# Causal attention of a twelve-layer decoder: row sums from a widened value tile, and a new quotient

## The reference, cut to what matters

```python
q = (x @ Wq_w.T + Wq_b).reshape(b, t, h, s).transpose(0, 2, 1, 3)   # kk, v alike; h = 16, s = 16
dot = jnp.einsum('bhqd,bhkd->bhqk', q, kk)
dot = jnp.where(causal, dot, -jnp.inf) / jnp.sqrt(256.0)
attn = jax.nn.softmax(dot, axis=-1)
out = jnp.einsum('bhqk,bhkd->bhqd', attn, v).transpose(0, 2, 1, 3).reshape(b, t, k)
return out @ Wo_w.T + Wo_b            # then x = layernorm(x + that)
```

## Time and profile before

| what | us |
|---|---|
| median of 3 runs | 3064.9 |
| the profiled execution | 3043.24 |
| its span | 3041.4 |
| TensorE busy in the span | 2806.5 (92%) |
| VectorE busy in the span | 1905.0 (63%) |
| ScalarE busy in the span | 1218.6 (40%) |
| TensorE records of L769, 512, mean 345 ns | 28.9 after overlap |
| TensorE records of L773, 512, mean 338 ns | 28.1 after overlap |
| VectorE reciprocal L960, 8, mean 3350 ns | 26.8 |

### The profile page before, as it was taken

One profiled execution on the slowest core, in us unless ns is written; L12 is line 12 of the kernel. 1 busy time (PEld: TensorE's weight loads), 2 busy tenths in 40 slices (PEclk: granted clock), 3 DMA queues, 4 the chain that ended last, 5 costly groups with the idle time before them and its releaser, 6 DMA issues. The chain is left out here.

```text
span 3041.4 us, 52348 instructions
## 1 busy us (share of the span) xinstructions
PE 2806.5 (92%) x20888; PEld 1815.5 (60%) x20888; DVE 1905.0 (63%) x3430; ACT 1218.6 (40%) x2591; POOL 324.8 (11%) x459
## 2 busy tenths in 40 slices
PE   6999899999998979899999989899898899989898
PEld 3565456666666858566666667656565333346576
DVE  4675367777764347477777753345557999966522
ACT  1333254445542335355544431133242866633111
POOL 1111100000002700000000000000111000001232
PEclk9999999999999979899999999999999999999899
DMA  3001000000012331100000000100000000000241
GB/s 117 20 14 69 23 33 5 5 5 5 5 67 78 92 127 37 42 5 5 8 6 5 36 18 1 33 17 21 19 21 32 18 1 1 1 18 18 101 168 66
DMA packets 43246, 103.58 MB, mean 34 GB/s; under 512 B 4929, under 2 KB 32687, under 8 KB 39425
## 3 DMA queue, kind: packets, MB, share of 16 engines
q1 hardware_dynamic: 37217, 86.66, 8.1%
q0 software_dynamic: 5792, 13.59, 1.5%
HBM read 66.74 MB, written 19.07 MB: 28 GB/s over the span
## 5 line engine op out<-in xcount | busy, mean ns | idle before, releaser
L2350 ACT ACTIVATE prob<-R,neg_max 128x333 f32<-128x333 f32 x512 | 268.7, 538 | 184.0 <-DVE neg_max L2417 183.8
L3898 DVE TENSOR_TENSOR_SCAN arena<-arena,u 128x512 f32<-128x512 f32 x256 | 289.5, 1200 | 0.3 <-issue 0.2
L2238 PEld LDWEIGHTS T<-const,prob 128*128 128x128 f32 (+1 forms) x1536 | 183.6, 143 | 82.4 <-DVE prob L2430 37.0
L2430 DVE TENSOR_TENSOR prob<-prob,rec 128x666 f32<-128x666 f32 x256 | 218.4, 853 | 19.8 <-issue 0.9
L2417 DVE TENSOR_REDUCE neg_max<-R 128x2 f32<-128x666 f32 x256 | 205.8, 845 | 34.9 <-PE R L2227 34.8
L2238 PE MATMUL T<-const,prob 128*128 128x128 f32 (+1 forms) x1536 | 211.0, 274 | 13.0 <-DVE prob L2430 10.7
L2357 ACT ACTIVATE prob_t<-T 128x384 f32<-128x384 f32 x256 | 125.8, 491 | 228.4 <-PE T L2238 222.3
L3829 ACT ACTIVATE arena<-delta,neg_a 128x510 f32<-128x510 f32 x256 | 174.5, 714 | 40.2 <-DVE arena L3898 39.1
L2423 DVE COPY prob_t<-T 128x384 f32<-128x384 f32 x256 | 142.3, 556 | 39.5 <-PE T L2238 13.0
L2157 PE MATMUL O<-keys_in,arena 128*128 128x333 f32 x512 | 164.8, 444 | 0.0
L3732 PE MATMUL R<-arena,diag 64*64 64x512 f32 x1024 | 136.0, 620 | 27.4 <-DVE arena L3898 27.3
(11 more groups left out here) (590 smaller groups left out, 5341.6 us busy)
## 6 DMA issues: line engine op xcount, KB each, us to landing
w<-w_dram SPq DMA_DIRECT2D x16, 1024.0 KB, 6.9
arena<-pack_dram SPq DMA_DIRECT2D x2, 4100.0 KB, 14.6
q_pad<-q_pad SPq DMA_DIRECT2D x24, 224.0 KB, 2.7
arena<-pack_dram SPq DMA_DIRECT2D x4, 1284.0 KB, 6.6
arena<-pack_dram SPq DMA_DIRECT2D x1, 4896.0 KB, 15.3
slots_in<-x_nat SPq DMA_DIRECT2D x2, 2048.0 KB, 8.7
arena<-planes SPq DMA_DIRECT2D x8, 512.0 KB, 8.5
arena<-k_nat SPq DMA_DIRECT2D x16, 224.0 KB, 2.7
```

The source lines that it names most:

```text
L2238: last = nc.tensor.transpose(S.T[0:n, i, kc * P:(kc + 1) * P], prob[:, g % 2, i, first:first + n], S.ident)
L2350: last = nc.scalar.activation(prob[:, g % 2, i, :], S.R[:, g % 2, i * BANK:i * BANK + XK], ACT.Exp, bias=neg_max[:, g % 2, i:i + 1], accum ...
L2430: nc.vector.tensor_tensor(prob[:, g % 2, :, :], prob[:, g % 2, :, :], rec[:, g % 2, :].unsqueeze(2).to_broadcast([P, 2, XK]), ALU.mult)\
L3898: nc.vector.tensor_tensor_scan(state[:, q % HELD, :], decay[:, q % DEEP, :], u[:, i % 2, :], 0.0, ALU.mult, ALU.add)\
```

## The change

The value tile is set to 1.0 instead of 0.0 once, so that the 16 unused columns of each head's 32 are ones. The product of a head with its tile then gives its 16 features and, in the other 16 partitions, its row sum. Even heads go to one bank (`S_one`), odd heads to the other (`S_two`), since they can no longer add up in one. The eight matmuls with `ones2` per call go, and `ones2` with its three memsets. ScalarE gets a new step `halves(b)`, between `keys(i+1)` and exponentials 0: it copies `S_one` times the mask `even` to `own`. VectorE's `quotient` becomes: transpose `S_two` in blocks of 32 x 32 to `turned`; after `halves_sb`, transpose `S_one`; `S_two * odd + own` to `attn_t`, which frees both banks (`sums_read`); reciprocal of the 32 sums of each token; a transpose of them, repeated 16 times, to `rec`; multiply. The next batch's product waits for `sums_read` in place of `attn_ready`.

```diff
@@ product @@
                     if t == 0:
                         pe.wait_ge(M.v_sb, b + 1)
                         if b >= 1:
-                            pe.wait_ge(M.attn_ready, b)
+                            pe.wait_ge(M.sums_read, b)
...
-                for s in range(2):
+                for s, sums in enumerate((S_one, S_two)):
                     for j in range(4):
-                        nc.tensor.matmul(S_num[32 * j:32 * j + 32, at], v2[:, b % 2, kt, 8 * t + 2 * j + s, :], exps_of(kt, t, j, s),
-                                         start=(t == 0 and kt == 0 and s == 0), stop=(kt == 1 and s == 1), skip_group_check=True)
-                for s in range(2):
-                    for j in range(4):
-                        last = nc.tensor.matmul(S_den[32 * j:32 * j + 32, at], ones2[:, s, :], exps_of(kt, t, j, s),
-                                                start=(t == 0 and kt == 0 and s == 0), stop=(kt == 1 and s == 1), skip_group_check=True)
+                        last = nc.tensor.matmul(sums[32 * j:32 * j + 32, at], v2[:, b % 2, kt, 8 * t + 2 * j + s, :], exps_of(kt, t, j, s),
+                                                start=(t == 0 and kt == 0), stop=(kt == 1), skip_group_check=True)
@@ scalar @@
+            def halves(b):
+                act.wait_ge(M.pv_full, b + 1)
+                if b >= 1:
+                    act.wait_ge(M.sums_read, b)
+                nc.scalar.activation(own[:], S_one, ACT.Copy, scale=even).then_inc(M.halves_sb, 1)
...
                     keys(i + 1)
+                if 0 <= i - 2 < B:
+                    halves(i - 2)
                 if 0 <= i - 1 < B:
                     exps(i - 1, 0)
@@ vector @@
             def quotient(b):
                 dve.wait_ge(M.pv_full, b + 1)
-                nc.vector.reciprocal(rec[:], S_den)
-                dve.drain()
-                nc.vector.tensor_tensor(attn_t[:, b % 2, :, :].rearrange("p c t -> p (c t)"), S_num, rec[:], ALU.mult)\
-                    .then_inc(M.attn_ready, 1)
+                nc.vector.transpose(turned[:, 1, :], S_two)
+                dve.wait_ge(M.halves_sb, b + 1)
+                nc.vector.transpose(turned[:, 0, :], S_one)
+                shares = attn_t[:, b % 2, :, :].rearrange("p c t -> p (c t)")
+                nc.vector.scalar_tensor_tensor(shares, S_two, odd, own[:], ALU.mult, ALU.add).then_inc(M.sums_read, 1)
+                sums = turned[:].rearrange("p s n -> p (s n)")[:, 16:2 * BANK - 16].rearrange("p (s n) -> p s n", s=2)[:, :, 0:BANK - 31:32]
+                dve.drain()
+                nc.vector.reciprocal(inverse[:].rearrange("p n s -> p s n"), sums)
+                dve.drain()
+                nc.vector.transpose(rec[:].rearrange("p (n s m) -> p n s m", s=2, m=16), inverse[:].unsqueeze(3).to_broadcast([P, 16, 2, 16]))
+                dve.drain()
+                nc.vector.tensor_tensor(shares, shares, rec[:], ALU.mult).then_inc(M.attn_ready, 1)
...
-            nc.vector.memset(ones2[:], 0.0)
-            nc.vector.memset(v2[:], 0.0)
-            dve.drain()
-            for s in range(2):
-                nc.vector.memset(ones2[:, s, 16 * s:16 * s + 16], 1.0)
+            nc.vector.memset(v2[:], 1.0)
+            dve.drain()
```

More of the change, by code:

```diff
@@ L630, in causal16 @@
         rstd = sb("rstd_own", [P, 2, TT])
-        ones2 = sb("ones2", [P, 2, 32])
+        own = sb("own", [P, BANK])
+        turned = sb("turned", [P, 2, BANK])
+        inverse = sb("inverse", [P, 16, 2])
         bq_s = sb("bq_s", [P, C])
-        S_q, S_y, S_num, S_den = S.T[:, 0, :], S.T[:, 1, :], S.O[:, 0, :], S.O[:, 1, :]
+        S_q, S_y, S_one, S_two = S.T[:, 0, :], S.T[:, 1, :], S.O[:, 0, :], S.O[:, 1, :]
         def bank(j):
@@ L809, in _ @@
                 if i < 2:
-                    keep_warm(nc, S, S_num, 1 + i)
+                    keep_warm(nc, S, S_one, 1 + i)
                 if now:
@@ L824, in _ @@
                     if i < 2:
-                        keep_warm(nc, S, S_num, 1)
+                        keep_warm(nc, S, S_one, 1)
                     scores(i, 1)
@@ L868, in _ @@
             settle(pe, M.attn_ready, B)
+            settle(pe, M.sums_read, B)
             settle(pe, M.y_read, B)
@@ L938, in _ @@
             bv = part(W, TB, "bv").rearrange("p (g m) -> p g m", m=32)
+            odd = part(S.const, CONST, "odd")
             def maxima(b, f):
@@ L1010, in _ @@
             settle(dve, M.pv_full, B)
+            settle(dve, M.halves_sb, B)
             settle(dve, M.y_full, B)
```

## The result

The changed kernel takes 3053.9 us (median of 15 runs, 3042.3 to 3067.7) against 3066.3 for the kernel before (15 runs, 3056.6 to 3083.6). The ratio is 0.9964, 95% interval 0.9948 to 0.998: between 6 and 16 us less, 11 in the middle. Times in us compare only within one measurement: beside e1 to e4 the kernel before took 3047.2, beside e5 to e8 3069.2, beside e9 to e12 3048.3.

A forecast was written before the change was run, and what follows sets the result against it. TensorE's own work, ending last in gaps 1 and 5, was taken as the bound. Loop 6.1 plus drain 3.1 made 9.2 us, less 2.2 for the clock: 7.0 off 3064.9, forecast 3057.9, range 3053 to 3067.

The forecast's parts named there:

- the drain: End of the causal block: earlier product start and fewer ones matmuls save 3.1 us, range 2.3 to 3.1.
- rival 1: Whole kernel: the clock holds, so the full 9.2 us is gained, giving 3055.7; chance 0.22.
- its larger loop term: Gap 5 of iterations 1 and 2: upper bound, two times 0.9 us more gained, giving 3053.9.
- iterations 1 and 2, gaps 1 and 5: Early loop: 0.49 us gained in gap 1 of iteration 2, 0.9 in gap 5 of each iteration.
- Gaps 1, 3 and 5: Between the loop's score groups: 0.87, 0.86 and 0.86 us of TensorE work go; 0.49, nothing and 0.47 are gained.
- The hand-over after gap 1: From the end of the maxima to the next score group: at least 0.05 us, as in gap 3.
- Rival 2: Loop: something other than TensorE holds the next group back; only the drain gains, 3.1 us, 3061.8; chance 0.14.
- rival 3: Loop, such as gap 3: the clock falls often, 2.67 us per slow stretch; with five, 3069.9; chance 0.14.
- Gap 5 at half clock: Iterations 1 and 2: 0.9 us gained in each, 1.8 together, from bounds of 0.47 and 1.79 each.
- Quotient, copy, queues: VectorE's new quotient, ScalarE's 0.69 us copy and moved queues cost 0; the quotient has 0.55 us of cover.
- The clock: Slow stretches take back 2.2 us: 0.8 in the drain, 1.35 in the loop in iteration 3 or 7.
- the price 0 of gap 3: Gap 3 of the loop: 0.86 us of TensorE work becomes a wait for the maxima, gaining nothing.

The follow-up runs named there:

- e1: Changed kernel with every product matmul issued twice: 3040.6 us against 3047.2 for the kernel before, ratio 0.9988.
- e4: Changed kernel with eight pairs of idle matmuls where TensorE waits longest in the causal block: ratio to the kernel before 0.9945.
- e5: Kernel before, unchanged, timed against itself: ratio 0.9992.
- e8: Changed kernel with the transpose of the first bank made three times, a quotient 1.6 us longer: one execution, 3075.6 us.
- e9: Kernel of e4 with more idle matmuls ahead of the second and third batch's scores in the next block: 3031.8 us against 3048.3 before, ratio 0.9946.
- e12: Changed kernel, unchanged, run again for a fourth profile; no total time or ratio of its own is given.
- e2: Kernel before with the ones matmuls issued for batch 0 alone: 3041.1 us against 3047.2 before, ratio 0.998.
- e7: The kernel of e4 measured again: ratio to the kernel before 0.9969.
- e10: Kernel before with the idle matmuls of e4 in the same places: 3044.3 us against 3048.3 before, ratio 0.998.

## Why the prediction was right

The direction and the mechanism of the gaps and of the drain were right, and the time lies in the range, 0.9 above its lower end: 3053.9 for a forecast of 3057.9 and a range of 3053 to 3067. That it lies inside is in part luck. The gain by the ratio is 11 us, not 7.0, and about 3 of it belong to no term of the sum. The time is also what rival 1 gives with its larger loop term, 3053.9, although its condition, that the clock holds, was not met: here the number alone would have named the wrong case. And absolute times move more between measurements than the 0.2% that the chances took: the kernel before had medians from 3047.2 to 3069.2. By terms, means of three profiles before and four after:

```
step                                 forecast   measured
start of block and iteration 0          0        -1.6
iterations 1 and 2, gaps 1 and 5       -2.3      -2.3
iterations 1 and 2, elsewhere           0        +1.7
iterations 3 to 5                      -2.9      -2.7
iteration 6                            -1.0      -0.3
maxima 0 of batch 7 to exponentials 0   0        +0.6
last exponentials 0 to last quotient   -3.1      -3.1
clock, unplaced                        +2.2      (in the rows above)
block                                  -7.0      -7.8
```

- **Gaps 1, 3 and 5.** Right: 0.87 and 0.86 of TensorE's time go, 0.40 and 0.47 are gained, nothing in gap 3. The hand-over after gap 1 was taken from gap 3 as 0.05 and is 0.15, hence 0.87 a full iteration and not 0.96. Rival 2 falls with this: after both gaps the bracket names the maxima. Of rival 3, falls in iterations 3 to 6, one came, in iteration 6.
- **Gap 5 at half clock.** Right in size: 1.8 forecast for iterations 1 and 2, 1.12 + 0.82 = 1.9 measured from maxima 2 to the next maxima 0. (The middle of the lower half of its bounds is 0.8, not the 0.9 taken; it doesn't matter.)
- **The drain** is right to 0.01 (14.84 measured, 17.93 - 3.08 = 14.85 worked out). The first block's 15.63, taken as the bound, held a fall of the clock: the same stretch of that block takes 14.77 or 14.78 in the seven profiles that have no half-clock time in it, and 15.05 to 15.67 in the seven that do.
- **Quotient, copy, queues.** Cost 0, shown by e2 against the changed kernel in iterations 3 to 5 and in the drain, and by e8 for the cover. In VectorE's queue the difference is -0.18, outside the bounds of -0.06 and +0.4, and it is hidden.
- **The clock.** That it takes part of the gain back was right, and 2.2 was near: 1.7 in iterations 1 and 2, 0.5 in iteration 6 (0.87 - 0.33) and 0.6 behind it make 2.8. Where it does so was wrong. I put 0.8 in the drain behind the last exponentials and the rest in iteration 3 or 7; the drain loses nothing, and iteration 3 never met a fall. The step that failed is the price 0 of gap 3: in iterations 1 and 2 the wait there grows from 0.52 to 1.38, and the stretch from maxima 1 to maxima 2, with a fall in it more often, is longer by 0.5 and 0.9 in the mean. With the waits of gaps 3 and 4 filled (e4, e7, e9) it is 7.73 again; gap 3 alone was not tried, so that its wait is the cause is argued; the profiles bear it out in iteration 2 (five of five against one of four), hardly in iteration 1. The other 0.3 of the 1.7 is gap 1 of iteration 1, where no product stands: a fall came there in two of the four profiles after and in one of the three before, which is chance.
- **Chance.** Iteration 0, where the clock falls in most profiles of both kernels, gave 1.3, and the start of the block 0.3. With the clock's 0.6 too much and the hand-over's 0.2 the sum ends 0.8 below the forecast, without the chance it would end 0.8 above it.
- **What the clock costs in all.** Against e4 and e7, the changed kernel with all but 7 us of half-clock time gone, its block is 8.0 longer (239.9 to 231.9), as much as the whole change is worth. About as much was lost before the change: 231.9 and the 8.0 of work that the table's rows at full clock add up to make 239.9 for the kernel before, an estimate, and it takes 247.7.
- **The total.** Of the 11 us by the timed ratio (6 to 16), the block explains 7.8. The next block is 3.0 shorter in the mean (132.5 to 129.5), but 129.3 to 137.3 before and 127.5 to 130.6 after overlap, and three profiles against four don't settle it. Its length changes with the block ahead, as e4, e7 and e10 show, so such a shift is possible; whether it is there stays open.

## What to carry to other kernels

Compare, gap by gap, the end of the work that frees a buffer with the start of the next use: TensorE time removed is worth only what that start is late, here 0.87 us of 2.6 per iteration, and all of it where the pipeline drains. When matmuls leave a program whose engine waits in short pieces, look at the granted clock of the thin iterations at both ends, and fill those waits, but only where the filler is shorter than the wait (in e10 it wasn't, and iterations 2 and 3 took 0.46 more), and look at the next block too. Judge by blocks over several profiles where a part that the change doesn't touch has two lengths 20 us apart.

## What the runs showed of the hardware

A small change in one block moved the half-clock stretches of the next reproducibly: 17 us in both profiles of the changed kernel with idle matmuls, 0 to 7 in the changed kernel's, and in e9, with the wait of 2.29 us filled, there were none. In the changed kernel TensorE waits 0.40, 0.80 and 0.32 in gaps 1, 3 and 5 of iterations 4 and 5, and 1.38 in gap 3 of iteration 3, and the full clock held there in all four profiles. In e8 the waits of gap 3 in iterations 3 to 6 were 1.99, 1.40, 1.41 and 1.40, and the clock fell 1.8 and 1.9 us behind the second and the fourth, not behind the longest. The Trainium skill (TensorE: Matmul & The Clock Gate, section "Why this matters for your kernels") ties falls to idle gaps between bursts; here they came behind waits of 1.84 and 1.06 (rows above), and in the kernel before a wait of 1.84 in the same place left the clock alone in two of three profiles. So the length of one wait doesn't decide by itself, and no run here shows what else does.
